# The last stage of layer 1 moved into the odd steps of layer 2, one batch ahead, with the batch loop written out

## What is computed

```
xn = layernorm(x)
x1 = x + attn0(xn) + (xn + routed(xn) + shared(xn))     # layer 1; routed: 2 of 16 experts a row
yn = layernorm(x1)
r  = yn / norm(yn) * sqrt(256) * (gamma + 1)
q, k, v = split(r @ w_qkv)                              # 16 heads of 64, 16 batches of 512 rows
o  = softmax(q k^T / 8) v                               # within a batch
out = x1 + o @ w_out + (yn @ ternary(w) * alpha + bias) # layer 2
```

## Time and profile before

| | us |
|---|---|
| median of the runs | 3274.73 (3274.7 to 3278.45) |
| profiled execution | 3273.24 |
| its span | 3271.2 |
| mean granted TensorE clock | 0.919 |

### The profile page before, as it was taken

How to read it: one execution, slowest core, us unless ns; L and a number is a source line. 1 busy time by engine, 2 the same in 40 slices (tenths; PEclk the granted TensorE clock), 3 DMA queues, 4 the chain that set the end, 5 groups by cost and what they waited for, 6 DMA issues and landing times.

```text
span 3271.2 us, 49812 instructions
## 1 busy us (share of the span) xinstructions
PE 2850.4 (87%) x14674; PEld 2360.9 (72%) x14674; DVE 2167.7 (66%) x3501; ACT 1883.7 (58%) x2746; POOL 2159.4 (66%) x1384
## 2 busy tenths in 40 slices
...
GB/s 115 90 95 84 66 60 125 181 176 204 217 215 168 40 62 61 64 73 44 70 60 63 74 47 66 60 63 74 47 68 58 63 74 47 71 55 63 74 51 48
DMA packets 266850, 281.11 MB, mean 86 GB/s; under 512 B 96754, under 2 KB 205554, under 8 KB 266739
## 3 DMA queue, kind: packets, MB, share of 16 engines
...
## 4 chain that ended last, share of the span: by engine, by line
PE 64%; DVE 1%; ACT 1%; POOL 1%; DMA 1%; issue 0%; SPq 0%; POOLq 0%; ACTq 0%; DVEq 0%
PE psV_b L1609 7%; PE psS_b L1597 7%; PE psV_b L1614 7%; PE psS_b L1596 7%; PE psV_b L1610 7%; PE psN_b L1582 7%; PE psY_b L1537 4%; PE psX_b L1537 4%; PE psY_b L1538 4%; PE psY_b L1539 4%; PE psX_b L1539 4%; PE psX_b L1538 4%; POOL pp_lo_b L1328 1%; PE psN_b L1666 0%; DMA xT_lo<-xT_lo_dram 0%
## 5 line engine op out<-in xcount | busy, mean ns | idle before, releaser
L1328 POOL TENSOR_TENSOR pp_lo_b<-pf_b,pp_hi_b 128x1024 fp32r<-128x1024 f32 x512 | 1228.4, 2399 | 605.3 <-ACT pp_hi_b L1370 518.1
L1473 DVE TENSOR_REDUCE negmax_b<-psN_b 128x2 fp32r<-128x1024 f32 x512 | 627.2, 1225 | 388.3 <-PE psN_b L1582 380.5
L1365 ACT ACTIVATE pf_b<-psS_b 128x1024 f32<-128x1024 f32 x512 | 525.9, 1027 | 239.9 <-PE psS_b L1597 236.7
L1596 PE MATMUL psS_b<-qA_b,kA_b 128*128 128x512 f32 x1024 | 406.1, 397 | 6.3 <-DVE qB_b L1488 4.4
L1597 PE MATMUL psS_b<-qB_b,kB_b 68*128 68x512 f32 x1024 | 406.7, 397 | 0.0
L1609 PE MATMUL psV_b<-pp_hi_b,vals_hi_b 128*128 128x512 f32 x1024 | 403.1, 394 | 1.6 <-DVE vals_lo_b L1505 0.3
L1610 PE MATMUL psV_b<-pp_hi_b,vals_lo_b 128*128 128x512 f32 x1024 | 402.8, 393 | 0.0
L1582 PE MATMUL psN_b<-kA_b,qA_b 128*128 128x512 f32 x1024 | 323.0, 396 | 4.6 <-DVE negmax_b L1473 4.4
L1614 PE MATMUL psV_b<-pp_lo_b,vals_hi_b 128*128 128x512 f32 x1024 | 318.1, 392 | 4.8 <-POOL pp_lo_b L1328 4.8
L1389 ACT ACTIVATE kA_b<-psX_b 64x512 fp32r<-64x512 f32 x256 | 151.8, 593 | 288.8 <-PE psX_b L1539 283.9
L1370 ACT ACTIVATE pp_hi_b<-pf_b 128x1024 fp32r<-128x1024 f32 x256 | 271.5, 1060 | 8.1
...
## 6 DMA issues: line engine op xcount, KB each, us to landing
kA_b<-kA_b SPq DMA_DIRECT2D x128, 256.0 KB, 3.0
qB_b<-qA_b SPq DMA_DIRECT2D x128, 256.0 KB, 2.9
inverse_b<-inverse_dram SPq DMA_DIRECT2D x256, 128.0 KB, 2.9
xs_e<-rows_dram SPq DMA_DIRECT2D x144, 128.0 KB, 2.0
results_dram<-ys_e SPq DMA_DIRECT2D x72, 256.0 KB, 2.3
...
part_dram<-acc_a SPq DMA_DIRECT2D x32, 256.0 KB, 2.2
acc_s<-part_dram SPq DMA_DIRECT2D x32, 256.0 KB, 3.7
```

Source lines behind the costliest of these rows:

```text
L1328: pool.tensor_tensor(pp[1][:, c], pf[:, c], pp[0][:, c].bitcast(F32), ALU.subtract).then_inc(pl_pool, 1)
L1365: a.activation(pf[:, c], psS[:], ACT.Exp).then_inc(exp_act, 1)
L1473: v.tensor_reduce(negmax[:, n.slot(2), 2 * c:2 * c + 2], psN[:], AX.X, ALU.max, negate=True).then_inc(mx_dve, 1)
L1596: pe.matmul(psS[:, t], kA[:, s, keys], qA[:, s], start=True, stop=False)
```

## The change

`settle` goes. Its work for a tile becomes pieces in the steps of `phase_b`, one batch ahead: while batch b is in its attention, the four tiles of batch b+1 are finished. PE's piece is a new kind of shared unit, "F", in the odd steps 1, 3, 9 and 11; it holds the four ternary matmuls of the tile before and the two transposes of this one. The pieces ahead of it are placed by `tile_at(g, d)`, d steps before the unit: POOL's add of `x` to the part sums and DVE's sums and statistics 4 steps before, POOL's powers 3 before, DVE's factors 2 before. `GATHERS` and `LOADS` place the gathers on POOL and the loads on SP. ACT normalises at the start of the unit's step and evicts the transposes behind the second exp. SP stores the result in the step behind (`put`), and the load of the next batch's `xT` in step 12 now waits for these stores (`ft_out`).

Output units take two tiles each, so four units of 24 matmuls a batch stand for eight of 12, with stores and `base_dram` loads of two tiles. The loop is written out, so each step is its own code. The steps begin at -24 in place of -3: the tiles of batch 0 are finished in steps -23 to -4. The splits of the weight chunks are spread over steps -20 to -1. The value tiles lose the copies of ones: 64 columns and one column of ones a head in the high part, 64 in the low part. The first weight chunk and gamma are loaded at the start of `experts`. What is computed stays.

```diff
-        SPLITS = {-4: range(0, 3), -3: [3, 4], -2: [5, 6], -1: [7]}
+        SPLITS = {-20: [0, 1], -13: [2], -8: [3, 4], -3: [5, 6], -1: [7]}
...
-        UNITS = {0: ("V", 0, 3), 1: ("O", -1, 2), 2: ("O", -1, 3), 3: ("V", 0, 4), 4: ("V", 0, 5),
-                 5: ("V", 0, 6), 6: ("V", 0, 7), 7: ("O", -1, 4), 8: ("O", -1, 5), 9: ("O", -1, 6),
-                 10: ("O", -1, 7), 11: ("O", 0, 0), 12: ("O", 0, 1), 13: ("V", 1, 0), 14: ("V", 1, 1),
-                 15: ("V", 1, 2)}
+        UNITS = {0: ("V", 0, 3), 1: ("F", 1, 0), 2: ("O", -1, 1), 3: ("F", 1, 1), 4: ("V", 0, 4), 5: ("V", 0, 5),
+                 6: ("V", 0, 6), 7: ("V", 0, 7), 8: ("O", -1, 2), 9: ("F", 1, 2), 10: ("O", -1, 3),
+                 11: ("F", 1, 3), 12: ("O", 0, 0), 13: ("V", 1, 0), 14: ("V", 1, 1), 15: ("V", 1, 2)}
+        FIRST = {1: 0, 3: 1, 9: 2, 11: 3}
...
+        GATHERS = {9: (0, 0), 10: (0, 1), 11: (1, 0), 12: (1, 1), 1: (2, 0), 2: (2, 1), 3: (3, 0), 4: (3, 1)}
+        LOADS = {12: 0, 14: 1, 3: 2, 6: 3}
...
-            for g in range(-3, H):
-                step(Step(None, H, g))
-            if B > 2:
-                with eng.Fori(1, B - 1) as it:
-                    for h in range(H):
-                        step(Step(it, H, h))
-            for g in range(H * (B - 1), NH + 11):
+            for g in range(-24, NH + 11):
                 step(Step(None, H, g))
...
+            def put(g):
+
+                u = unit(g + -1)
+                if u is None or u[0] != "F":
+                    return
+                n = TB * u[1].const + u[2]
+                if n < NT:
+                    at = slice(n % TB * P, (n % TB + 1) * P)
+                    need(sp, f_act, 1, n, 1)
+                    sp.dma_start(xT_hi[n // TB, :, :, at], ft[0][:].bitcast(F32)).then_inc(ft_out, 16)
+                    need(sp, f_dve, 1, n, 1)
+                    sp.dma_start(xT_lo[n // TB, :, :, at], ft[1][:].bitcast(F32)).then_inc(ft_out, 16)
+                if n > 0:
+                    m = n - 1
+                    need(sp, fb_dve, 1, m, 1)
+                    sp.dma_start(base_dram[m // TB, :, m % TB, :], fsum[:, m % 3]).then_inc(base_out[m // TB % 2], 16)
...
             def step(g):
                 p = q_unit(g)
+                if g.const == -10:
+                    for c in range(len(STAGES), len(chunks)):
+                        sp.wait_ge(w_dve, KD * (c - len(STAGES) + 1))
+                        load_weights(c)
+                put(g)
...
                     after(sp, kq_pe, 2, pair_at(g, 2), 2)
+                    sp.wait_ge(ft_out, 32 * TB * (batch(g, 1).const + 1))
                     load_x(batch(g, 1))
...
+                n = tile_at(g, 4)
+                if n is not None:
+                    pool.wait_ge(sums_in[n % 3], 16 * (n // 3 + 1))
+                    pool.wait_ge(fx_in, 16 * (n + 1))
+                    pool.tensor_tensor(fsum[:, n % 3], fsum[:, n % 3], fx[:], ALU.add).then_inc(fx_pool, 1)
                 p = pair_at(g, -5)
                 if g.const % 2 == 1 and p.within(0, NP):
...
+                n = tile_at(g, 3)
+                if n is not None:
+                    need(pool, s_dve, SD, n, 4)
+                    need(pool, s_dve, SD, n - 2, SD)
+                    pool.tensor_tensor(mv[:, n % 2, 2:3], mv[:, n % 2, 1:2], eps, ALU.add).then_inc(s_pool, 1)
+                    need(pool, s_pool, 2, n, 1)
+                    pool.tensor_tensor(root[:, n % 2], mv[:, n % 2, 1:3], power, ALU.pow).then_inc(s_pool, 1)
...
-                    pe.matmul(psV[:, g.slot(2)], values(0, h, i), pp[0][:, c, t], start=(i == 0), stop=False)
-                    pe.matmul(psV[:, g.slot(2)], values(1, h, i), pp[0][:, c, t], start=False, stop=False)
+                    pe.matmul(psV[0:DH + 1, g.slot(2)], values(0, h, i), pp[0][:, c, t], start=(i == 0), stop=False)
+                    pe.matmul(psV[0:DH, g.slot(2)], values(1, h, i), pp[0][:, c, t], start=False, stop=False)
...
+                        n = TB * b.const + number
+                        if n > 0:
+                            need(pe, f_dve, 1, n - 1, 1)
+                            for k in range(KD):
+                                pe.matmul(psY[:, 0, D:2 * D], ft[0][:, k], kept.wtern[:, k], start=(k == 0), stop=False)
+                                mm = pe.matmul(psY[:, 0, D:2 * D], ft[1][:, k], kept.wtern[:, k], start=False, stop=(k == KD - 1))
+                        if n < NT:
+                            if n == 0:
+                                pe.wait_ge(const_dve, 3)
+                            need(pe, fr_act, 1, n, 1)
+                            for k in range(KD):
+                                mm = pe.transpose(psY[:, 0, k * P:(k + 1) * P], fr[:, k * P:(k + 1) * P], ident[:].bitcast(F32))
+                        mm.then_inc(f_pe, 1)
```

More of the change, by code:

```diff
@@ L106, in need, with route @@
         eng.wait_ge(sem, per * n + k)
-def route(nc, io, rows, part, region, jobs, kept, raw, raw_in):
+def route(nc, io, rows, part, region, jobs, kept, order, raw, raw_in):
     x_dram = io["x"].rearrange("(g t p) d -> g p t d", t=TB, p=P)
@@ L279, in const @@
                 own[0] += 1
-            for tile, value in ((kept.ident[:], 0.0), (masks[:, 0], 0.0), (masks[:, 1], 1.0), (masks[:, 2], 1.0), (masks[:, 3], 1.0)):
+            for tile, value in ((order.ident[:], 0.0), (masks[:, 0], 0.0), (masks[:, 1], 1.0), (masks[:, 2], 1.0), (masks[:, 3], 1.0)):
                 const(g.memset(tile, value))
@@ L717, in _ @@
                             three(out, [part[:, u % XT, t, k] for part in xt], [part[:, k] for part in wshare], k == 0, False)
-                        pe.matmul(out, kept.pick[:], bshare[:], start=False, stop=False)
+                        pe.matmul(out, order.pick[:], bshare[:], start=False, stop=False)
                         for h in range(FH):
@@ L735, in _, with experts @@
                     pe.matmul(psB[:, 0, 0:1], masks[:, 3], delta[:, 0:1], start=True, stop=True).then_inc(tern_pe, 1)
-def experts(nc, io, rows, results, region, jobs, kept, raw, raw_in):
+def experts(nc, io, rows, results, region, jobs, early, kept, order, raw, raw_in):
     with ExitStack() as ctx:
@@ L879, in _ @@
                     j = n * U + t
[L880 removed]
+                    at = pe.value_load(order.table[0:1, j:j + 1], min_val=0, max_val=(NE - 1) * D)
                     out = psY[:, n % 3, t * D:(t + 1) * D]
[L882 removed]
+                    pe.matmul(out, order.pick[:], brow[:, bass.ds(at, D)], start=True, stop=False)
                     for k in range(KD):
@@ L1093, in phase_b @@
-def phase_b(nc, io, xT_hi, xT_lo, base_dram, early):
+def phase_b(nc, io, xT_hi, xT_lo, base_dram, results, part_dram, early, kept):
     B = base_dram.shape[0]
@@ L1134, in phase_b @@
         negmax = sb("negmax", [P, 2, TB], F32R)
+        fsum = sb("fsum", [P, 3, D])
+        fx = sb("fx", [P, D])
+        fy = sb("fy", [P, 2, TOP, D])
+        fr = sb("fr", [P, D])
+        ft = [sb(f"ft_{p}", [P, KD, P], F32R) for p in ("hi", "lo")]
+        fbias_bc = sb("fbias_bc", [P, D])
+        columns = sb("columns", [P, 32])
+        power, eps, stats = columns[:, 0:2], columns[:, 2:3], columns[:, 4:10]
+        mv, root = [columns[:, at:at + 2 * n].rearrange("p (r n) -> p r n", r=2) for at, n in ((10, 3), (16, 2))]
+        fac = columns[:, 20:32].rearrange("p (r n) -> p r n", r=3)
         psN = bank("psN", 2)
@@ L1254, in spread_sums @@
                         .then_inc(spread_in[j], 16)
-            for c in range(1, len(chunks)):
-                if c >= len(STAGES):
-                    sp.wait_ge(w_dve, KD * (c - len(STAGES) + 1))
+            for c in range(1, len(STAGES)):
                 load_weights(c)
@@ L1514, in step @@
                 if g.const % 2 == 1:
                     row()
+                if unit(g) is not None and unit(g)[0] == "F":
+                    k = TB * unit(g)[1].const + unit(g)[2]
+                    if k > 0:
+                        if k == 1:
+                            v.wait_ge(bias_in, 16)
+                        need(v, fb2_dve, 1, k - 1, 1)
+                        v.tensor_tensor(fsum[:, (k - 1) % 3], fsum[:, (k - 1) % 3], fbias_bc[:], ALU.add).then_inc(fb_dve, 1)
                 done = pair_at(g, -3)
@@ L1521, in step @@
                     v.reciprocal(spread[:, r], spread[:, r]).then_inc(nm_dve, 1)
+                m = tile_at(g, 4)
+                if m is not None:
+                    total = fsum[:, m % 3]
+                    need(v, fx_pool, 1, m, 1)
+                    v.wait_ge(gathered[m % 2], 16 * TOP * (m // 2 + 1))
+                    for k in range(TOP):
+                        need(v, s_dve, SD, m, k)
+                        v.scalar_tensor_tensor(out=total, in0=fy[:, m % 2, k], scalar=kept.share[k][:, m:m + 1],
+                                               in1=total, op0=ALU.mult, op1=ALU.add).then_inc(s_dve, 1)
+                    need(v, s_dve, SD, m, 2)
```

(4 more changed lines are left out.)

462 lines of the change are left out of this document (190 added, 272 removed).

## The result

The changed kernel takes **3528.95 us** (3525.88 to 3532.48, 4 runs), the one before 3276.59 us in the same session (3274.7 to 3280.46, 4 runs): **1.0769** times as long, 95% interval 1.075 to 1.0788. It is 252 us slower where the forecast said 28 us faster, and it lies outside the range.

The account below looks back on a forecast made before the run. PE was taken to bound the second layer. 3273.2 - 249 (lead-in) + 45 (PE's added work) + 177 (stalls) = 3246, and 1.5 for the median: 3247 us, range 3125 to 3310.

Parts of the forecast that it names:

- Lead-in, 249 us gone: Before the first score matmul: 326.6 us go and a lead-in of 78 us comes, so 249 us less (235 to 260).
- PE, 3.0 us a batch: Second layer on PE: two transposes and four matmuls a tile add 0.75 us, 45 us over 15 batches.
- The 65 and 64 columns: Value matmuls on PE: narrower weights stream the same 512 columns, so 0; 30 us at best was not excluded.
- POOL and SP: Steps of `phase_b`: PE waits for later POOL adds and later SP loads and copies, 10.4 us a batch.
- DVE, "1.4 a batch together, an estimate from the rows of `settle`": Batches of `phase_b`: added DVE work delays `kB` and, in steps 3, 9 and 11, the mask row, 1.4 us a batch.
- rival B: Slower: the stall in step 13 lowers PE's clock in each batch, 3.3 us more each, 3297 us; chance 0.28.
- Rival A: Second layer takes the tiles at little over PE's price, 4.7 us of stalls a batch, 3141 us; chance 0.22.
- C: Lead-in is not short, since tiles 2 and 3 hang on weights: 110 us instead of 78, 3279 us; chance 0.08.

Follow-up runs that it names:

- the repaired kernel: Changed kernel with one-tensor-input factor operations behind the mask row, and SP's loads, stores and `kA` reordered: 3233.41 us, 0.9854 of the kernel before.

## Why the prediction was wrong

- **Lead-in, 249 us gone: right.** 800.0 for the first projection and 823.6 for the first score, predicted 800 and 824.
- **PE, 3.0 us a batch: right for the matmuls.** In the repaired kernel the starts of a tile's four ternary matmuls lie 0.12 us apart, as predicted. At 1.00 the repaired batch has 143.1 busy where 135.4 + 3.0 were due; the 4.7 more are not explained by any matmul that was added, and may be the records around its waits. The 65 and 64 columns gave nothing: their matmuls still start 0.23 us apart.
- **POOL and SP: most places right, the sizes within a microsecond but for step 1.** Step 13: `xT_lo` 0.87 and `pp_lo` 3.83, with 1.4 and 4.0 predicted. Step 5: `kA` 2.14 for 1.7. Step 15: 0.59 for 0.9. Step 1: 0.24 for 1.7. Steps 7 and 9: nothing for 0.9 and 0.3. Not named: 0.85 for `kA` in step 13. Together, with a small one for the maxima (0.43), 9.0, of which the kernel before had 0.5: 8.5 for the 10.4 predicted. That the sum is near is in part luck, since misses both ways cancel in it. The add of 128x256 took 0.73, as put down, though the half of L1000 that the prediction names for it is 0.63.
- **DVE, "1.4 a batch together, an estimate from the rows of `settle`": the step that failed.** It was 9.1 for the mask row alone, at the end of steps 15, 1, 7 and 9 and not of 3, 9 and 11. I took the four small operations at their lengths where they ran beside nothing, and moved them to a place where POOL's `pp_lo` runs for 4.8 of each 8.5 us. A price has to be read with the neighbour that the new place has. A pair of rows of the kernel before, DVE and POOL in `settle`, could have warned. L1060 has two tensor inputs; its mean is 183 ns, and here it ends with POOL's add (767.41 and 767.38):

```profile
766.19 1.22 DVE L1060 TENSOR_TENSOR fac_s<-root_s 128x2 f32<-128x2 f32 x1 [4.83 <-POOL root_s L998]
```

```profile
766.13 1.25 POOL L1000 TENSOR_TENSOR x1b_s<-x_s,fbias_bc_s 128x512 f32<-128x512 f32 x1
```

  No DVE operation in the batches of `phase_b` before had two inputs in SBUF. But the cast L1483, with one, hinted that POOL can hold DVE there: 240 of its 256 began inside POOL's operation, took 0.74 to 1.32 us and ended 0.55 behind it; the 16 others took 0.68. The Trainium skill (SBUF — State Buffer, Who interferes with whom) says that a DVE instruction with two SBUF inputs contends with a GpSimd instruction that reads SBUF, and that the later one blocks until the first has finished. The trace agrees: in four kernels the held operations shown ended within 0.03 us of POOL's. I did not look this rule up for the operations that the change moves.
- **The clock: rival B was the true mechanism, and too small.** I priced it in one place, behind one wait of 4 us, at 3.3 a batch. In the batch shown it fell behind all six waits over 2 us, 11.9 us, and the idles of that batch add to 18.3. With 18.3 for 11.8 and 11.9 for 3.3, each batch is 15.1 us longer than in B, and 3297 + 15 x 15.1 = 3524. That this comes so near to 3529 is luck: with the mean of the fourteen whole batches, 19.4 and 10, it is 3297 + 15 x 14.3 = 3512, and 17 us are open. The sentence that fixed its condition ("if the wait of step 13 comes out as long as that idle", 4.44 us) took the one row I had for a lower bound. That row also cost less than I read from it, since its stretch of 6.7 us began at 1064.70 and PE worked again only at 1066.96. And the point from which the kernel is slower is 204 / 15 = 13.6 us a batch, not 13.4. The Trainium skill (TensorE: Matmul & The Clock Gate, Loop structure matters more than you think) warns of waits between bursts; the runs show it from 1.58 us on, in most cases, and not at 1.1.
- **Rival A** (141 to 143 us a batch) was not reached: the repaired version has 150.6 in the mean. **C** did not happen.

The chance of 0.33 for slower was fair to B as I saw it; the range was not, since it stopped at 12.7 us of stalls a batch and gave the clock one place.

**To carry over.** When small operations move to another engine's busy stretch, list for each how many of its tensor inputs lie in SBUF, and look at what POOL runs there: with two, its length was that of what was left of POOL's operation, though it had one column. A `tensor_scalar` with the second value as a per-partition scalar does the same work unheld. And count waits on a busy TensorE by their length: in the changed kernel 55 of the 70 that lasted 2 us or more were paid a second time in clock, in the last one 6 of 9 between 1.58 and 1.99, so a repair that shortens such waits can give back more than their idle.
